# Attention with LayerNorm on one core: gamma and beta go into two VectorE operations

## What is computed

```python
q, k, v = (x_seq @ w + b for w, b in ...)          # 16 x 900 x 512, 8 heads of 64
scores = einsum('bhqd,bhkd->bhqk', q, k) / 8 + spatial_bias[|dh| + |dw|]
ctx = einsum('bhqk,bhkd->bhqd', softmax(scores), v)
resid = ctx @ wo + bo + x_seq
mu, var = mean(resid, -1), mean((resid - mu) ** 2, -1)
out = (resid - mu) * rsqrt(var + 1e-5) * ln_gamma + ln_beta
```

## Time and profile before

| | |
|---|---|
| time, median of 3 runs | 3438.34 us |
| the profiled execution | 3438.66 us, span 3436.8 us, mean granted TensorE clock 0.977 |
| TensorE matmul busy | 3164.5 us (92%) |
| VectorE busy | 2557.5 us (74%) |
| ScalarE busy | 2781.2 us (81%) |
| GpSimd busy | 1683.3 us (49%) |
| stretch 2257 to 2374 us (units 26 to 59 of one image) | TensorE busy 111.18 of 117 us, GpSimd 35.28 |
| stretch 2169 to 2257 us (units 0 to 25 of it) | TensorE busy 83.34 of 88 us, GpSimd 69.78 |
| stretch 3376 to 3437 us (the end) | TensorE busy 32.95 of 61 us, GpSimd 50.01, granted clock 0.80 |

### The profile page before, as it was taken

How to read it: one execution, slowest core, us unless ns; L and a number is a source line. 1 busy time by engine, 2 the same in 40 slices (tenths; PEclk the granted TensorE clock), 3 DMA queues, 4 the chain that set the end, 5 groups by cost and what they waited for, 6 DMA issues and landing times.

```text
span 3436.8 us, 127113 instructions
## 1 busy us (share of the span) xinstructions
PE 3164.5 (92%) x52744; PEld 2150.3 (63%) x52744; DVE 2557.5 (74%) x5461; ACT 2781.2 (81%) x7015; POOL 1683.3 (49%) x3305
## 2 busy tenths in 40 slices
PE   3899999999999999999999999999999999999986
PEld 2566666666666666666666666666666666666654
DVE  2577878777787777878777786877778777786875
ACT  2698787888878888787888978888797888878783
POOL 0124627355372644727355372644627355372647
PEclk7999999999999999999999999999999999999998
DMA  5232322323232232322323232232322323232220
GB/s 153 64 83 61 93 77 61 95 61 95 69 86 80 68 93 61 93 76 62 95 61 96 68 89 77 69 92 66 89 81 66 90 57 96 66 89 77 69 64 23
DMA packets 317939, 267.44 MB, mean 78 GB/s; under 512 B 109913, under 2 KB 240985, under 8 KB 317361
## 3 DMA queue, kind: packets, MB, share of 16 engines
q1 hardware_dynamic: 172242, 130.32, 14.5%
q10 hardware_dynamic: 145120, 129.00, 12.4%
HBM read 193.73 MB, written 63.66 MB: 75 GB/s over the span
## 4 chain that ended last, share of the span: by engine, by line
PE 37%; POOL 18%; ACT 17%; DVE 15%; DMA 5%; SPq 4%; issue 3%; ACTq 0%; DVEq 0%; POOLq 0%
PE pv_ps L689 10%; PE s_ps L670 9%; ACT prob L787 7%; PE r_ps L587 7%; PE r_ps L605 7%; ACT prob L803 6%; DVE prob L919 5%; DMA other<-own 5%; POOL tokens L1072 4%; POOL tokens L1074 4%; DVE prob_t L932 4%; SPq L474 3%; POOL tokens L1056 2%; POOL weight L1029 2%; DVE stats L945 2%
## 5 line engine op out<-in xcount | busy, mean ns | idle before, releaser
L919 DVE CUSTOM_DVE_ANT_0 prob<-s_ps,window 128x450 f32<-128x450 f32 x1920 | 1126.7, 625 | 586.3 <-PE s_ps L670 490.9
L787 ACT ACTIVATE prob<-prob,own 128x450 f32<-128x450 f32 x1920 | 1266.1, 662 | 298.1 <-DVE own L919 295.7
L803 ACT ACTIVATE prob<-prob,weight 128x450 f32<-128x450 f32 x1920 | 1172.1, 659 | 80.0 <-POOL weight L1029 80.0
L932 DVE STREAM_TRANSPOSE prob_t<-prob 128x960 f32<-128x960 f32 x960 | 1124.4, 1171 | 62.4 <-ACT prob L803 54.9
L670 PE MATMUL s_ps<-k_sb,q_sb 64*32 64x450 f32 x15360 | 864.2, 552 | 85.5 <-DVE own L919 84.2
L689 PEld LDWEIGHTS pv_ps<-prob_t,values 64*64 64x64 f32 x30720 | 769.2, 136 | 227.6 <-issue 169.8
L689 PE MATMUL pv_ps<-prob_t,values 64*64 64x120 f32 x30720 | 824.9, 263 | 29.2 <-ACT ctx_sb L813 26.4
L587 PE MATMUL r_ps<-xt,w_sb 128*128 128x450 f32 x3072 | 710.1, 378 | 16.4 <-ACT q_sb L743 10.6
L587 PEld LDWEIGHTS r_ps<-xt,w_sb 128*128 128x128 f32 x3072 | 565.3, 190 | 153.6 <-issue 74.3
L1015 POOL TENSOR_TENSOR lead<-own,other 128x4 f32<-128x4 f32 x480 | 96.7, 201 | 913.1 <-DMA other<-own 912.9
L670 PEld LDWEIGHTS s_ps<-k_sb,q_sb 64*32 64x32 f32 x15360 | 228.4, 106 | 480.7 <-issue 304.2
(11 more groups left out here) (58 smaller groups left out, 1630.2 us busy)
## 6 DMA issues: line engine op xcount, KB each, us to landing
w_sb<-w_split ACTq DMA_DIRECT2D x126, 512.0 KB, 4.1
values<-v_dram ACTq DMA_DIRECT2D x256, 240.0 KB, 3.1
tokens<-in_x SPq DMA_DIRECT2D x214, 240.0 KB, 3.5
other<-own SPq DMA_DIRECT2D x1920, 1.0 KB, 2.1
out<-tokens SPq DMA_DIRECT2D x105, 240.0 KB, 3.0
v_dram<-stage SPq DMA_DIRECT2D x96, 240.0 KB, 2.8
v_dram<-stage SPq DMA_DIRECT2D x32, 180.0 KB, 2.5
tokens<-in_x SPq DMA_DIRECT2D x30, 120.0 KB, 3.2
```

The lines of the kernel that those rows point to most:

```text
L787: nc.scalar.activation(prob[:, u % RING, head, 0:HALF], prob[:, u % RING, head, 0:HALF], ACT.Exp, scale=-1.0, bias=own[:, s, 0, c:c + 1], ...
L803: nc.scalar.activation(prob[:, u % RING, head, 0:HALF], prob[:, u % RING, head, 0:HALF], ACT.Copy, scale=weight[:, s, c:c + 1]).then_inc(p ...
L919: nc.vector.tensor_tensor_reduce(prob[:, u % RING, head, 0:HALF], s_ps[:, u % 2, head, 0:HALF], window[:, w0:w0 + HALF // GRID, :].rearran ...
L932: nc.vector.transpose(out=prob_t[:, g % 2, v % PER_GROUP, :, :].rearrange("p h k -> p (h k)"), in_=prob[:, u % RING, :, :].rearrange("p h ...
```

## The change

GpSimd's `scale_shift` is removed with its two products per tile, and so is its wait for gamma and beta ahead of the loop. VectorE's tensor_scalar becomes two scalar_tensor_tensor operations. The first stands at the end of `out_sum`, at unit e: it subtracts the mean and multiplies by gamma. It waits for bn_aggr. The second stands in `out_norm`, at unit e+2: it multiplies by the reciprocal root and adds beta, and its semaphore is the one that the store waits for. GpSimd still computes the root.

```diff
                 nc.vector.bn_aggr(mean_var[0:m, i, :], stats[0:m, i, :]).then_inc(mean_done, 1)
+                dve.wait_ge(mean_done, n)
+                nc.vector.scalar_tensor_tensor(out=y, in0=y, scalar=mean_var[0:m, i, 0:1], in1=gamma_all[0:m, :],
+                                               op0=ALU.subtract, op1=ALU.mult).then_inc(centred, 1)
 
             def out_norm(im, work):
...
+                dve.wait_ge(centred, n)
                 dve.wait_ge(rstd_done, n)
-                nc.vector.tensor_scalar(y, y, mean_var[0:m, i, 0:1], rstd[0:m, i:i + 1],
-                                        ALU.subtract, ALU.mult).then_inc(normed, 1)
+                nc.vector.scalar_tensor_tensor(out=y, in0=y, scalar=rstd[0:m, i:i + 1], in1=beta_all[0:m, :],
+                                               op0=ALU.mult, op1=ALU.add).then_inc(shifted, 1)
...
-            def scale_shift(im, work):
-                t, n = work[1], out_no(im, work) + 1
-                m, y = rows(t), y_of(t, work[0] == "final")
-                pool.wait_ge(normed, n)
-                nc.gpsimd.tensor_tensor(y, y, gamma_all[0:m, :], ALU.mult).then_inc(scaled, 1)
-                pool.wait_ge(scaled, n)
-                nc.gpsimd.tensor_tensor(y, y, beta_all[0:m, :], ALU.add).then_inc(shifted, 1)
-
-            pool.wait_ge(small_in, 16 * 3)
-
...
-                for work in im.out_tiles(u - 2):
-                    scale_shift(im, work)
```

More of the change, by code:

```diff
@@ L386, in attention_layernorm @@
         rstd_done = sem("rstd_done")
-        normed = sem("normed")
-        scaled = sem("scaled")
+        centred = sem("centred")
         shifted = sem("shifted")
@@ L947, in out_sum @@
                 nc.vector.bn_aggr(mean_var[0:m, i, :], stats[0:m, i, :]).then_inc(mean_done, 1)
+                dve.wait_ge(mean_done, n)
+                nc.vector.scalar_tensor_tensor(out=y, in0=y, scalar=mean_var[0:m, i, 0:1], in1=gamma_all[0:m, :],
+                                               op0=ALU.subtract, op1=ALU.mult).then_inc(centred, 1)
             def out_norm(im, work):
-                t = work[1]
-                i, m, n = t % SLOTS, rows(t), out_no(im, work) + 1
-                y = y_of(t, work[0] == "final")
+                t, n = work[1], out_no(im, work) + 1
+                i, m, y = t % SLOTS, rows(t), y_of(t, work[0] == "final")
+                dve.wait_ge(centred, n)
                 dve.wait_ge(rstd_done, n)
-                nc.vector.tensor_scalar(y, y, mean_var[0:m, i, 0:1], rstd[0:m, i:i + 1],
-                                        ALU.subtract, ALU.mult).then_inc(normed, 1)
+                nc.vector.scalar_tensor_tensor(out=y, in0=y, scalar=rstd[0:m, i:i + 1], in1=beta_all[0:m, :],
+                                               op0=ALU.mult, op1=ALU.add).then_inc(shifted, 1)
             for t in range(NT):
```

## The result

| | median | lowest to highest |
|---|---|---|
| before, 8 runs | 3436.99 us | 3432.56 to 3446.77 |
| after, 8 runs | 3457.47 us | 3448.55 to 3466.61 |

The ratio is 1.0058, with a 95% interval of 1.0040 to 1.0075. The changed kernel is slower by some 20 us. The forecast was 3427 us, faster, with a range to 3446: wrong in sign and outside its range. The profiled execution of after took 3460.25 us with a span of 3458.4.

A forecast was written before the change was run, and what follows sets the result against it. TensorE, busy 92%, was taken as the bound, waiting for VectorE, which waits for GpSimd's bias addition. From 3438.66 us, +3 for 15 steady images and -14.5 for the last image's end gave 3427 us, range 3406 to 3446.

The forecast's parts named there:

- Place A: Units 8 to 11 of a steady image: relief almost cancelled by added operations, -0.15 us, +1.0 with 0.3 us blocking.
- Place B: Units 14 to 17, with 0.5 us to spare: VectorE 1.2 us late, TensorE loses 0.65 us, 1.55 with full blocking.
- Place C: Units 19 to 21: the sum's 2.62 us wait for its bias addition goes, and TensorE's 0.70 us wait with it.
- The cost of the operations: VectorE's two new operations: 0.69 us long each, adding 0.72 and 0.15 us, 0.87 per tile before blocking.
- The row at 2215.36: Profile row cited for blocking: the old tensor_scalar took 1.36 us beside a GpSimd subtraction of 1.22 us.
- the upper end of the blocking: 0.3 us of blocking by GpSimd on each new VectorE operation, expected by the skill's rule; tied to chance 0.12.
- 0.1 more each: Blocking by GpSimd taken for each new VectorE operation: 0.1 us more, from a range of 0 to 0.3.
- The relief: GpSimd loses two products per tile, about 330 us of 1683; only what is queued behind them counts.
- The end: Last image's output tiles, after its attention: a chain of GpSimd, VectorE and TensorE steps, -14.5 us, range -10 to -18.
- Rival 2: VectorE becomes the bound, its new operations blocked behind GpSimd's root and split, 0.3 us each: 3452 us, chance 0.12.
- rival 1: Cancelled gain: blocking of about 0.2 us each costs the images +15 us against -14.5: 3439 us, chance 0.2.
- One sign of being wrong: TensorE's waits for VectorE above 110 us in all, one of three results named as refuting the forecast.

The follow-up runs named there:

- relief_only: Kernel before without GpSimd's two products, nothing in their place, so gamma and beta are not applied; 0.9759 of the kernel before, 83 us faster.
- extra_op: bias_first plus, per steady tile, the change's first scalar_tensor_tensor into a spare buffer nobody reads; 1.0125 of the kernel before, 3486.16 us.
- bias_first: final_only with GpSimd's bias addition and reciprocal root moved ahead of its two products at each unit; 0.9790 of the kernel before, 3365.24 us.
- final_only: Kernel before with the two scalar_tensor_tensor for the last image's eight tiles alone; 0.9960 of the kernel before, 14 us faster.
- the halves: The change made in the last image's eight tiles alone, 0.9960, and in the 120 steady tiles alone, 1.0057, each against the kernel before.

## Why the prediction was wrong, point by point

- **What bounds the kernel.** Right in words (VectorE reaches TensorE at A, B and C), wrong in weight. I took VectorE's work in the output stretch as mostly covered by its waits for TensorE. The experiments with and without that work (relief_only against after, extra_op against bias_first) say that it costs nearly its whole time, with the half clock in it.
- **The cost of the operations.** The row at line 888 was the right one but for its scalar, which I noted and then priced at nothing: 0.75, not 0.69. What the first one adds between the sum and the transpose is 2226.68 - 2224.32 = 2.36 us against 1.54 before, 0.82 and not 0.72; the second adds 0.20 and not 0.15. A slip in the sum besides: 0.1 us of blocking on the seven operations of A and B makes -0.2 to about +0.5 us an image, not +0.2, so +7 us and not +3.
- **Blocking.** The Trainium skill's rule ("SBUF — State Buffer", Who interferes with whom) holds for the new form, and in both directions: at 2220.52 the new operation took 1.47 us behind a GpSimd subtraction begun 0.31 us earlier (0.72 more than its median, of the 0.91 that the subtraction still ran), and at 2250.21 the addition of epsilon took as long as the new operation beside it. The row at 2215.36, which I gave for it, is no case of it: the old tensor_scalar has one tensor as its input. I named the rule and gave the upper end of the blocking a chance of 0.12. In the mean over all tiles it is 0.12 and 0.06 us, my "0.1 more each". But it sits where it hurts: the first operation of tile 1 is blocked in 11 of 15 images, that of tile 2 in 9, the second of tile 1 in 5, those of the other tiles never but once. They meet GpSimd's split of the context and bias addition. The old tensor_scalar had such a pattern too: its mean of 638 ns was tile 3 alone, 1.36 us in all 15 images. A mean over tiles was the wrong measure.
- **Place A, the failed step.** I put it at -0.15 us, up to +1.0 with full blocking. The idle column says +1.0 (the wait grew from 1.22 to 2.24 us); the starts say more. From the context matmuls of unit 7 to those of unit 14 TensorE takes 28.7 us in the images of before (28.7 to 29.0) and 31.6 in the mean of the 15 images after (29.7 to 32.4): **+2.8 us**. A fit over the 15 images, by the time that the three operations above took beyond their medians and by whether there is a half-clock stretch, gives 0.25 us in every image, 1.0 us for each us of block, and 1.6 us for the stretch, and leaves under 0.2 us in any image. In the mean that is 0.25 us for the longer chain (0.4 above my -0.15; relief and cost do almost cancel), **1.2 us of blocks, priced at 0.1 each, and 1.4 us of half clock, priced at nothing**.
- **Place B.** +0.65 to +1.55 forecast. From unit 14 to 18 TensorE falls back by 1.06 us in 14 of 15 images. Right.
- **Place C.** -0.70 forecast. TensorE's wait is gone and it regains 0.94 there and 0.6 in the two pairs of units that follow, 1.54 in all. Right in kind, and twice the size.
- **What was missing.** The half clock. No rival had it, though the earlier trace rows shows a granted clock of 0.80 at the end and I used it there. Place A pays 1.4 us an image for it; fewer stretches elsewhere give a part back, so that some 13 of the 31 us are its share and the other 18 are blocks and longer operations. Without any change in the half clock the images would still have cost 18 us, not 3, and the kernel would have stood near 3444 us, an estimate, still slower than before. Two images of after are wholly at 1.00: the one at 2818.2 us takes 204.3 us, as long as the image shown of before (204.4, also at 1.00), and the one at 1360.4 us takes 207.3, with 1.5 us of blocks at A and a wait of TensorE of 3.09 us near B.
- **The relief.** I let the cost eat the relief at A and so never priced it alone. Alone it is 83 us, of which the end is about 19 (30.1 us behind the last transpose in place of 48.8); bias_first shows that it needed an order, not another engine.
- **The end.** -14.5 us forecast, -14 by the ratio of final_only, 34.1 us in place of 48.8 behind the last transpose. The two late steps came as said: the matmuls of the last tiles, forecast 5.5 us earlier, start at 3443.84, which is 19.5 us behind the last transpose in place of 24.9, and the last operation ends at 3455.67, 2.7 us before the end of the span of 3458.4:

```profile
3437.15 5.82 PE L629 MATMUL r_ps<-wo_sb,ctx_split 128*120 128x512 f32 x24 [2.85 <-POOL ctx_split L1048]
...
3443.84 5.83 PE L629 MATMUL r_ps<-wo_sb,ctx_split 128*120 128x512 f32 x24 [0.87 <-POOL ctx_split L1048]
...
3452.95 2.72 DVE L956 SCALAR_TENSOR_TENSOR last_tokens<-last_tokens,rstd,beta_all 120x512 f32<-120x512 f32 x4
```

  TensorE's gap before the last tiles is 0.87 us where it was 3.93, and its 24 matmuls take 5.8 us, not 7.2.
- **The rivals and their chances.** Rival 2 (VectorE as the bound, blocked behind GpSimd's root and split, 3452 us) is what happened, at 0.12. That its price was near is partly luck: it put +1.55 us at B, which got 1.06, and +1.0 at A, which got 2.8, and it had no half clock. Against rival 1 I held that the root and splits fall where VectorE does transposes; they fell beside the new operations. One sign of being wrong came true, TensorE's waits for VectorE above 110 us (113.0).

Left open: what the blocking costs outside place A, since no kernel here had the new operations without GpSimd's reads beside them; why the same wait is followed by the low clock in 13 images and not in 2; and why the halves by themselves sum to less than the whole.

## What to carry to other kernels

Price a wait of TensorE by the distance between the starts of its blocks and ask what clock follows it; at place A the idle column grew by 1.0 us and the distance by 2.8. Look at blocking tile by tile, not in the mean, and at which tiles stand on the path. Count the half clock in both kernels before giving a difference to it. Where an engine's delay ends in a short step of another engine's list, move that step forward in the list before moving work between engines: here the order of three calls gave 58 us, which the removal of 330 us of work also gave, but at a higher cost on VectorE. And when an edit both relieves and loads, price each alone; a sum of two large terms with opposite signs has the error of both.

## What the runs showed of the hardware

- A scalar read from a column makes scalar_tensor_tensor 60 ns longer than a number does (752 against 692 ns, 748 against 686, 120x512 float32).
- Behind an idle 2.24 us of TensorE the granted clock fell to 0.50 for 3.4 us in 13 of 15 images and stayed at 1.00 in 2; behind 2.04 us (extra_op) it fell in 9 of 15; behind 1.22 us at the same place, and with matmuls in the wait, in none. It cost 1.6 us each time.
- VectorE with two SBUF inputs and GpSimd hold each other up even where GpSimd's operation is one column wide: 0.19 us became 0.64 in the mean beside a new operation, and up to 0.75. At place A each us of such blocks made TensorE 1.0 us late.
